# Values of eight slots together in the near tiles of a relative-position attention and MoE kernel

## The reference, cut to what matters

```python
B, S, D = 16, 512, 128      # 16 heads of 8, M = 128
q, k, v = proj(Wq, bq), proj(Wk, bk), proj(Wv, bv)        # of layernorm(x)
idx = clip(r[None, :] - r[:, None], -M, M) + M
content  = einsum('bhqd,bhkd->bhqk', q, k)
relative = einsum('bhqd,qkd->bhqk', q, rel_k[idx])
w = softmax((content + relative) / sqrt(8))
out = einsum('bhqk,bhkd->bhqd', w, v) + einsum('bhqk,qkd->bhqd', w, rel_v[idx])
x = x + layernorm(out.reshape(B, S, D) @ Wo.T + bo)
x = x + layernorm(moe(layernorm(x)))                       # 16 experts, top 1, and a shared one
```

## Time and profile before

| | |
|---|---|
| runs | 1652.87, 1658.00, 1658.12 us; median 1658.0 us |
| span of the profiled execution | 1623.4 us |
| own time of the profiled execution | not listed apart; the median is 34.6 us above the span |
| one turn, 4th of 8 | 162 us |
| TensorE busy | 1522.4 us |
| VectorE busy | 1229.5 us |
| ScalarE busy | 1112.7 us |

### The profile page before, as it was taken

How to read it: one execution, slowest core, us unless ns; L and a number is a source line. 1 busy time by engine, 2 the same in 40 slices (tenths; PEclk the granted TensorE clock), 3 DMA queues, 4 the chain that set the end, 5 groups by cost and what they waited for, 6 DMA issues and landing times.

```text
span 1623.4 us, 67801 instructions
## 1 busy us (share of the span) xinstructions
PE 1522.4 (94%) x28642; PEld 1184.3 (73%) x28642; DVE 1229.5 (76%) x3459; ACT 1112.7 (69%) x2053; POOL 472.2 (29%) x585
## 2 busy tenths in 40 slices
PE   5889999999999999999999999999999999899993
PEld 2337877787778777877777777777777776568992
DVE  7996668787878887888788878787877235644996
ACT  4437777777777777777777777777766776237881
POOL 4432020223122313231313131313101101664567
PEclk9899999999999999999999999999999999999996
DMA  3468657775565446544644464456424673425551
GB/s 85 144 189 223 149 146 165 181 184 140 113 152 110 121 110 149 111 131 100 154 103 126 104 156 98 122 112 143 97 57 102 124 207 75 121 90 150 162 167 51
DMA packets 489136, 212.10 MB, mean 131 GB/s; under 512 B 330663, under 2 KB 462436, under 8 KB 488832
## 3 DMA queue, kind: packets, MB, share of 16 engines
q1 hardware_dynamic: 474112, 165.74, 44.4%
q0 software_dynamic: 14720, 42.03, 7.5%
HBM read 105.73 MB, written 102.85 MB: 128 GB/s over the span
## 4 chain that ended last, share of the span: by engine, by line
PE 75%; DVE 15%; issue 4%; DMA 2%; ACT 1%; POOL 1%; SPq 1%; ACTq 0%; DVEq 0%; POOLq 0%
PE pv L867 14%; PE mix L822 12%; PE sc L845 9%; DVE mx L1381 8%; PE rel L874 8%; PE sc L847 7%; PE mix L824 7%; PE sc L839 4%; PE sc L1030 2%; PE rel L976 1%; POOL out_dram L1977 1%; PE sc L966 1%; PE pv L967 1%; PE mix L884 1%; ACT w L1122 1%
## 5 line engine op out<-in xcount | busy, mean ns | idle before, releaser
L1122 ACT ACTIVATE w<-sc,escale 128x512 f32<-128x512 f32 x1024 | 686.1, 688 | 310.9 <-PE sc L847 188.3
L1381 DVE TENSOR_REDUCE mx<-mix 128x1 f32<-128x512 f32 x960 | 643.3, 684 | 201.4 <-PE mix L824 191.5
L822 PE MATMUL mix<-WE 128*32 128x512 f16 (+1 forms) x1968 | 386.3, 392 | 25.0 <-DVE mx L1381 14.4
L867 PE MATMUL pv<-w,shared_part 128*9 128x128 f32 x8192 | 371.4, 273 | 3.6 <-issue 3.6
L824 PE MATMUL mix<-Wn,WE 128*32 128x384 f16 (+3 forms) x1968 | 295.2, 304 | 0.0
L845 PEld LDWEIGHTS sc<-shared_part,Wt 96*128 96x128 f16 x5120 | 223.3, 97 | 84.1 <-issue 30.9
L845 PE MATMUL sc<-shared_part,Wt 96*128 96x64 f16 x5120 | 259.0, 193 | 4.2 <-DVE mx L1381 1.9
L867 PEld LDWEIGHTS pv<-w,shared_part 128*9 128x9 f32 x8192 | 204.1, 90 | 78.2 <-issue 48.9
L874 PE MATMUL rel<-w,shared_part 128*32 128x128 f32 x5120 | 257.5, 273 | 0.6 <-issue 0.6
L847 PE MATMUL sc<-shared_part 104*128 104x128 f16 x2560 | 248.7, 219 | 1.0 <-issue 1.0
L1107 ACT ACTIVATE WE<-qp,hmask 128x256 f16<-128x256 f16 x500 | 215.6, 499 | 23.5 <-PE sc L824 23.5
(11 more groups left out here) (263 smaller groups left out, 1926.4 us busy)
## 6 DMA issues: line engine op xcount, KB each, us to landing
qm_d<-ks POOLq DMA_DIRECT2D x48, 512.0 KB, 4.5
shared_part<-qm_d SPq DMA_DIRECT2D x32, 768.0 KB
kt_d<-ks SPq DMA_DIRECT2D x48, 256.0 KB
shared_part<-kt_d SPq DMA_DIRECT2D x128, 96.0 KB
xs_d<-zrow SPq DMA_DIRECT2D x5, 2056.0 KB, 11.4
vs_d<-vst SPq DMA_DIRECT2D x16, 576.0 KB
shared_part<-vs_d SPq DMA_DIRECT2D x32, 288.0 KB
orl_d<-rel_s SPq DMA_DIRECT2D x512, 8.0 KB
```

The source lines that it names most:

```text
L822: nc.tensor.matmul(nat[rows, :], lq[:, rows], kn[b2][:, KEYS_AT[t]:KEYS_AT[t] + S], start=True, stop=False, skip_group_check=True)
L867: mm = nc.tensor.matmul(pv[b2][32 * g:32 * g + 9, P * hh:P * hh + P], VC[j][:, b2, 0 if near else 1, h, :], wt[:, :, b2, h, :], start=(j = ...
L1122: nc.scalar.activation(weights, products, ACT.Exp, scale=escale[:, 0:1]).then_inc(s["exp_done"], 1)
L1381: nc.vector.tensor_reduce(mx[:, k:k + 1], nat[:], AX.X, ALU.max).then_inc(s["mx_done"], 1)
```

## The change

In near tiles of key block 1 or more (tiles 0.1, 1.1, 1.2, 2.1, 2.2, 2.3, 3.2 and 3.3) `slots_together` gives 8 and not 4. Near tiles of key block 0 keep 4, far tiles 2. TensorE then issues eight slots' scores and natural scores and behind them eight values; ScalarE's masked copies of these tiles follow behind the eighth exponential. Nothing else is moved by hand, and nothing is added or left out.

```diff
     def slots_together(slot, nxt):
 
-        return 4 if nxt and abs(slot // 32 - slot // 8 % 4) <= 1 else 2
+        if not nxt or abs(slot // 32 - slot // 8 % 4) > 1:
+            return 2
+        return 8 if slot % 32 >= 8 else 4
...
                 due = (slot,)
-                if slots_together(slot, nxt) == 4:
-                    due = range(slot - 3, slot + 1) if slot % 4 == 3 else ()
+                together = slots_together(slot, nxt)
+                if together > 2:
+                    due = range(slot - together + 1, slot + 1) if slot % together == together - 1 else ()
                 for earlier in due:
```

## The result

The changed kernel takes 1701.1 us (median of six runs, 1696.7 to 1707.9), the kernel before beside it 1658.1 (1652.9 to 1661.8). The ratio is **1.0259, 95% interval 1.0234 to 1.0284**: 43 us slower. The forecast was 1689 in a range from 1666 to 1704: the sign and the mechanism held, the cost was 12 us too low.

What follows compares the result with a forecast made beforehand. TensorE's instruction stream was taken as the bound (busy 94%). Per full turn, 5.05 + 0.8 + 0.7 + 0.6 - 1.76 = +5.4; in all +31 us on 1658.0 gives 1689, range 1666 to 1704.

Steps and rivals of the forecast that it cites:

- Saved, 0.22 per tile and 12.3 in all: One entry and one exit of the column-tiled values less per near tile, 56 tiles: 12.3 us saved.
- Waits for row maxima in tiles 1.1, 1.2 and 3.2: TensorE's natural scores wait for VectorE's row maxima: 1.6, 1.2 and 0.8 us per turn.
- Tile 2.3, 1.45: Slots 94 and 95 wait for row maxima 92 and 93: 1.45 us per turn.
- Copies: ScalarE's copies in eights: waits of 0.8 in tile 3.3, 0.7 in tile 2.2, nothing behind near values.
- the moved step: Slot 123: TensorE's transpose of finished tokens waits 0.6 us for VectorE's normalisation, with no four values between.
- Tile 2.1, put at nothing for row maxima: Little on VectorE in the stretch of tile 2.1 that counts, so no row max wait there.
- About +1: Turn 0 has no second half to finish, emptying tiles 1.1 and 1.2, so it costs about +1 us.
- I take the 34.6 as unchanged: The gap between the profiled span, 1623.4, and the runs' median, 1658.0, was assumed to stay.
- Hidden waits: Rival: finishing steps slide into the values' time, only the saving stays, 1646 us; chance 0.09.
- the draw: Rival: waits are a quarter of those worked out, 1.8 per turn, and eat the saving, 1658 us; chance 0.06.
- ScalarE as the worse one: Rival: exponentials behind eight copies also hold up tiles 1.3 and 0.2, +14 us, 1703; chance 0.07.
- The clock: Rival: waits bring a fall to 1.2 GHz for 3% of each turn, 35 us more, 1724; chance 0.03.

Runs made afterwards that it cites:

- the pair of short reciprocals: VectorE's reciprocals over one column of 128: in the changed kernel 1676.4 us (1.0120), in the kernel before 1654.2 us (0.9989).
- copies_in_eights_only: The kernel before with values still in fours but ScalarE's masked copies in eights in the same eight tiles: 1685.6 us, 1.0169.
- after_finish_moved: The changed kernel with the second half's finishing steps four slots later and the first half's last three reciprocals at slots 93 to 95: 1689.5 us, 1.0206.
- before_again: The kernel before, unchanged, run again for a second profile: 1662.6 us.
- copies_in_fours: The changed kernel, values in eights, with ScalarE's masked copies back in fours: 1719.3 us, 1.0369.
- after_short_pool: The changed kernel with POOL's subtraction over a quarter of its elements: 1687.6 us, 1.0195.

## Why the prediction was right, and where its size was off

**Saved, 0.22 per tile and 12.3 in all: right.** Tile 0.1, where nothing else changes, is 0.22 shorter in every full turn. The page "TensorEngine Tiling (Array Packing)" of the Trainium skill says, under Key Properties, that a change of mode drains the TensorE; the estimate of 0.33 from the Trainium skill's "TensorE: Matmul & The Clock Gate", Single matmul latency, is not borne out: the switch costs the 0.22 of the rows.

**Waits for row maxima in tiles 1.1, 1.2 and 3.2: right** to 0.2 each. Tile 1.1 goes slot by slot as worked out, and the pair of short reciprocals shows the cause. Behind tiles 1.2 and 3.2 no experiment stands by itself: their sizes fit, and shorter reciprocals leave them alone, as they should. The trace has the same sign there: in turn 3 the natural scores of slots 53, 54 and 118 start at 692.60, 694.22 and 777.15, each 0.05 to 0.06 behind the end of row max 51, 52 and 116.

**Tile 2.3, 1.45: the term that was mis-sized.** Gross of the saving it cost 1.35 to 4.4 in turns 1 to 5. The step that failed is "Slot 94 wants row max 92 (724.22)": it took VectorE's operations behind row max 91 at their lengths in the trace of before. Moved against POOL's preparing steps, one of them took up to 1.8 us longer, and in turns 2 and 4 a fall of the clock followed. Over the whole program the tile cost 12.9 net of the saving, where about 7.4 was forecast.

**Copies: right** in tiles 2.2 and 3.3 (+0.50 and, with the moved step, +1.22). Costing them at nothing behind near values was right for tiles 0.1 and 1.2: the tiles behind them, 0.2 and 1.3, keep their length in turns 2 to 6, and copies_in_eights_only, where both grow, shows that the cover is the eight values.

**Tile 2.1, put at nothing for row maxima: wrong by 0.3** (+0.07 for -0.22). The loss is in slot 78, 1.36 for 1.02: in turn 3 its natural scores start at 722.58, 0.05 behind the end of row max 76 (721.84 + 0.69), which VectorE had come to late, behind three of the second half's finishing steps. With those steps moved (after_finish_moved) the tile keeps its 0.22.

**Turn 0.** "About +1" doesn't follow from emptying tiles 1.1 and 1.2 alone, which leaves +2.6; measured, turn 0 got 2.5 shorter. Against before_again, tile 1.3 grew by 2.2 in turns 0 and 1 together, and turn 7, which keeps its twos, by 2.6; these weren't forecast and aren't explained.

**The base.** The sum was added to the median of 1658, as the metric wants. "I take the 34.6 as unchanged" was wrong in its reason (1.8 lie around a span), and did no harm, since only the median entered.

**The rivals.** Hidden waits and the draw are out: tiles 1.1, 1.2, 2.3 and 3.2 grew by 30.2 us together over the program, net of their saving, and the waits of natural scores' weight loads alone rose by 24.4 or 31.6, where some 30 were named. ScalarE as the worse one fails by place: tile 0.2 doesn't change, and tile 1.3 only in turns 0 and 1 of the seven with eights. **The clock** was dismissed by turn 0's row. There TensorE's longest idle stretch is 2.08 us, the others 1.0 or less, and the clock stays at 1.00. In the turns of the changed kernel it did fall, twice, not for 3% of each turn but behind the two longest waits there, 2.27 and 2.46 us: about 2 us in all by the table above, not 35. Of the signs named, slot 40 to slot 48 is 1.4 longer, slot 122 waits for an exponential, and turn 3 takes 169.6, not 162 or less.

## What to carry to other kernels

Grouping work on one engine to save a switch takes away the pauses in which the engines behind it catch up: set the switches saved (here 0.22 a tile) against what the followers do in those pauses (here four steps of 0.94 on VectorE), not against their average slack. Where two banks allow a lead of two slots, a burst of eight runs at the follower's pace once the lead is used up (here 1.40 a slot for 0.85 in tile 1.1). When work shifts in time, ask also what a third engine does at the new moment, and move work that was held for the same cover (here the masked copies) along with the cover.

## What the runs showed of the hardware

A small VectorE operation can last as long as POOL's large one: 128 by 16 elements took 1.77 and 1.98 us for 0.23 and 0.17, ending within 0.04 us of a POOL subtraction of 2.12 and 2.16. The Trainium skill, "SBUF — State Buffer", Who interferes with whom, says that a VectorE instruction with two SBUF inputs contends with a GpSimd instruction that reads SBUF; the trace agrees: both of those operations have two inputs, and in turn 2 the next one runs at once after POOL's end. Two such inputs are not needed for it: in copies_in_fours, turn 5, a TENSOR_SCALAR with one (L1565, 128 by 16) took 2.17 us for 0.23, ending 0.04 behind a subtraction of 2.12.

TensorE's granted clock fell from 1.00 to 0.52 behind a wait of 2.27 us in turn 2 of the changed kernel. The length of one wait doesn't settle whether it falls. First after_short_pool, turn 2, then copies_in_fours, turn 5: the wait, and a window behind it.

```profile
570.94 0.43 PE L824 MATMUL mix<-WE 128*128 128x512 f16 x1 [1.30 <-DVE mx L1384]
...
572.70:576.10 3.40, 3.40 (x66) 2.73 (x68) 1.92 (x5) 0.02 (x1) 0.00 (x0) 0.52 0.97 364
```

```profile
1100.03 0.44 PE L824 MATMUL mix<-WE 128*128 128x512 f16 x1 [2.25 <-DVE mx L1384]
...
1101.00:1104.00 3.00, 2.00 (x30) 1.27 (x32) 3.00 (x6) 1.38 (x2) 0.00 (x0) 1.00 1.02 369
```

Behind 1.30 us the clock fell to 0.52, behind 2.25 it stayed at 1.00; what decides is open. Turn 0, busy for 153 of 162 us, didn't bring it down either.

The same program's last stretch took 254.8 us in one execution and 280.0 in another.
